# Storing a convolution's results group by group, with one transfer for both regions of an image

## The reference

```python
xn = group_norm(x)                       # 32 groups of 2 channels
pooled = xn.mean(axis=(2, 3))
a = relu(pooled @ fc1_w.T + fc1_b)
att = softmax(a @ fc2_w.T + fc2_b)       # four weights for each image
agg_w = einsum('bk,koihw->boihw', att, weight)   # an own 3x3 kernel for each image
agg_b = att @ bias
out = x + conv3x3(xn, agg_w) + agg_b     # stride 1, padding 1
```

## Time and profile before

| | |
|---|---|
| median of three runs | 313.08 us (312.87 to 314.52) |
| the profiled execution | 314.18 us |
| its span in the trace | 312.3 us |
| TensorE, products | 297.9 us busy, 95% of the span |
| TensorE, weight loads | 266.2 us, 85% |
| VectorE | 246.5 us, 79% |
| ScalarE | 189.8 us, 61% |
| GpSimd | 22.9 us, 7% |
| bytes moved by DMA | 53.62 MB, 172 GB/s over the span |

### The profile page before, as it was taken

How to read it: one execution, slowest core, us unless ns; L and a number is a source line. 1 busy time by engine, 2 the same in 40 slices (tenths; PEclk the granted TensorE clock), 3 DMA queues, 4 the chain that set the end, 5 groups by cost and what they waited for, 6 DMA issues and landing times.

```text
span 312.3 us, 15651 instructions
## 1 busy us (share of the span) xinstructions
PE 297.9 (95%) x7029; PEld 266.2 (85%) x7029; DVE 246.5 (79%) x760; ACT 189.8 (61%) x241; POOL 22.9 (7%) x32
## 2 busy tenths in 40 slices
PE   7299998999999999999999999999999999999994
PEld 5256866778787989999987998899999999999993
DVE  2988897888999998999798989889696987856000
ACT  1292937739194676738386868767684866767321
POOL 1004040040400000000000000000000000000000
PEclk9779999999999999999999999999999999999999
DMA  7893084480946658482936869495664416070564
GB/s 254 329 395 108 2 266 150 121 290 13 279 139 221 197 171 245 135 250 58 295 106 185 233 161 238 128 240 176 173 188 136 135 35 178 2 195 18 144 171 105
DMA packets 19283, 53.62 MB, mean 172 GB/s; under 512 B 7568, under 2 KB 10896, under 8 KB 19216
## 3 DMA queue, kind: packets, MB, share of 16 engines
q1 hardware_dynamic: 18912, 52.41, 56.6%
q10 hardware_dynamic: 304, 0.22, 0.3%
HBM read 26.89 MB, written 25.69 MB: 168 GB/s over the span
## 4 chain that ended last, share of the span: by engine, by line
PE 75%; DVE 10%; ACT 8%; issue 3%; DMA 2%; SPq 0%; DVEq 0%; ACTq 0%
PE acc L793 75%; DVE stats L324 2%; ACT o L675 2%; DMA x<-x 2%; DVE mix L436 2%; ACT xh L623 2%; ACT x L605 2%; ACT wh L653 1%; DVE xl L512 1%; ACT xh L631 1%; ACT wh L640 0%; DVE wparts L343 0%; DVE x L520 0%; DVE mix L434 0%; DVE mv L332 0%
## 5 line engine op out<-in xcount | busy, mean ns | idle before, releaser
L793 PE MATMUL acc<-xh,wh 64*64 64x385 f16 (+3 forms) x2304 | 112.1, 326 | 1.3 <-ACT xh L623 0.7
L793 PE MATMUL acc<-xl,wh 64*64 64x385 f16 (+3 forms) x2304 | 111.1, 325 | 0.6 <-issue 0.4
L793 PE MATMUL acc<-xh,wl 64*64 64x385 f16 (+3 forms) x2304 | 110.6, 325 | 0.6 <-issue 0.6
L675 ACT ACTIVATE o<-acc,out_par 128x392 f32<-128x392 f32 x127 | 78.2, 669 | 52.9 <-PE acc L793 52.7
L793 PEld LDWEIGHTS acc<-xh,wh 64*64 64x64 f16 x2304 | 87.8, 107 | 12.0 <-ACT wh L653 1.6
L793 PEld LDWEIGHTS acc<-xl,wh 64*64 64x64 f16 x2304 | 90.9, 107 | 7.7 <-issue 1.3
L793 PEld LDWEIGHTS acc<-xh,wl 64*64 64x64 f16 x2304 | 87.8, 107 | 10.2 <-issue 1.0
L324 DVE BATCH_NORM_STATS2 stats<-x 128x6 f32<-128x448 f32 x112 | 64.9, 615 | 5.2 <-DMA x<-x 5.2
L631 ACT ACTIVATE xh<-x,xof,xsc 128x1568 f16<-128x1568 f32 x24 | 40.5, 1690 | 32.3 <-DVE xof L398 32.3
L512 DVE TENSOR_TENSOR xl<-x,xh 128x1568 f16<-128x1568 f32 x28 | 49.9, 1785 | 8.1 <-ACT x L605 7.9
L436 DVE SCALAR_TENSOR_TENSOR mix<-w_sb,ex,mix 128x192 f32<-128x192 f32 (+1 forms) x72 | 44.2, 614 | 0.9
(11 more groups left out here) (60 smaller groups left out, 135.6 us busy)
## 6 DMA issues: line engine op xcount, KB each, us to landing
x<-x SPq DMA_DIRECT2D x30, 784.0 KB, 6.5
out<-o SPq DMA_DIRECT2D x30, 392.0 KB, 5.0
out<-o SPq DMA_DIRECT2D x30, 294.0 KB, 4.6
out<-o SPq DMA_DIRECT2D x44, 98.0 KB, 3.5
out_par<-par SPq DMA_DIRECT2D x64, 0.5 KB, 2.0
x<-x SPq DMA_DIRECT2D x2, 448.0 KB, 4.9
x<-x SPq DMA_DIRECT2D x3, 224.0 KB, 6.2
w_sb<-w_t SPq DMA_DIRECT2D x2, 288.0 KB, 4.9
```

The source lines that it names most:

```text
L675: nc.scalar.activation(o_sb[i][m][:, g * GN:(g + 1) * GN], acc[n % SLOTS][m][:, 0:GN], ACT.Identity, bias=out_par[i][m][:, 1:2], scale=out ...
L793: ins = nc.tensor.matmul(pixels[:, top:bottom, left:right], weights[i][halves[m], tap * C:(tap + 1) * C], window, start=start and step == ...
```

## The change

All pairs are now stored group by group. `group_of(p, g, m)` gives the two sides of one transfer: in DRAM a view of the image as eight bands, [band, channel, pixel], of which it takes the group's upper and lower band by a slice with a step; in SBUF all 128 rows of `o_sb` at the group's 392 columns. So a pair has eight stores of 128 rows x 392 pixels where it had six of 64 rows, and the last group is stored by one transfer for each image instead of two. The load of pair p+4 is cut into quarters of 784 pixels; quarter g is issued behind the stores of group g of pair p. The parameters of pair p+1 are issued between the stores of group 2 and the quarter behind them. The counts that the waits at L323 and L673 look for follow: 64 for a tile loaded in quarters, 64 for a pair's four stores of an image.

```diff
--- before.py
+++ after.py
@@ -194,17 +194,19 @@
             else:
                 engine.wait_ge(s_xh[half], p - EARLY + 1)
 
+        def group_of(p, g, m):
+
+            bands = out_d[2 * p + m].rearrange("c (b n) -> b c n", n=GN)
+            upper, lower = BANDS[0][g], GROUPS + BANDS[1][g]
+            return bands[upper:lower + 1:lower - upper], o_sb[p % 2][m][:, g * GN:(g + 1) * GN]
+
         block = ctx.enter_context(nc.Block())
 
         @block.sync
         def _(sp):
-            def load(p, half):
-                if p >= X_RING:
-
-                    for n in range(2):
-                        sp.wait_ge(s_xl[n], p - X_RING + 1)
+            def first_load(p, half):
                 pixels = slice(half * HALF, (half + 1) * HALF)
-                sp.dma_start(x_sb[p % X_RING][:, pixels], x_d[p, :, pixels]).then_inc(x_in[p % X_RING], 16)
+                sp.dma_start(x_sb[p][:, pixels], x_d[p, :, pixels]).then_inc(x_in[p], 16)
 
             def spread_params(p):
                 i = p % 2
@@ -213,23 +215,17 @@
                     for r in range(2):
                         sp.dma_start(out_par[i][m][halves[r], :], par[i][halves[m], :]).then_inc(s_outp[i], 16)
 
-            def store(p, m):
-                i = p % 2
-                sp.wait_ge(s_res, 2 * GROUPS * p + 2 * (GROUPS - 1) + m + 1)
-                image = out_d[2 * p + m]
-
-                sp.dma_start(image[:, 0:GN], o_sb[i][m][halves[0], HALF - GN:HALF]).then_inc(stored[i][m], 16)
-                sp.dma_start(image[:, GN:HALF], o_sb[i][m][halves[0], 0:HALF - GN]).then_inc(stored[i][m], 16)
-                sp.dma_start(image[:, HALF:PIX], o_sb[i][m][halves[1], :]).then_inc(stored[i][m], 16)
+            def load_quarter(p, n):
+
+                for half in range(2):
+                    sp.wait_ge(s_xl[half], p - X_RING + 1)
+                pixels = slice(n * HALF // 2, (n + 1) * HALF // 2)
+                sp.dma_start(x_sb[p % X_RING][:, pixels], x_d[p, :, pixels]).then_inc(x_in[p % X_RING], 16)
 
             def store_group(p, g):
-                i = p % 2
                 for m in range(2):
                     sp.wait_ge(s_res, 2 * GROUPS * p + 2 * g + m + 1)
-                    for r in range(2):
-                        first = r * HALF + BANDS[r][g] * GN
-                        sp.dma_start(out_d[2 * p + m, :, first:first + GN],
-                                     o_sb[i][m][halves[r], g * GN:(g + 1) * GN]).then_inc(stored[i][m], 16)
+                    sp.dma_start(*group_of(p, g, m)).then_inc(stored[p % 2][m], 16)
 
             for n, (first, last) in enumerate(PIECES):
                 pixels = slice(first * CHUNK, last * CHUNK)
@@ -241,30 +237,22 @@
             sp.wait_ge(s_weights[0], 16)
             for p in range(1, X_RING):
                 for half in range(2):
-                    load(p, half)
+                    first_load(p, half)
             spread_params(0)
-            for p in range(PAIRS - 1):
-
-                if p + X_RING < PAIRS:
-                    load(p + X_RING, 0)
-                spread_params(p + 1)
-                if p + X_RING < PAIRS:
-                    load(p + X_RING, 1)
-                for m in range(2):
-                    store(p, m)
-            for g in range(GROUPS - 1):
-                store_group(last_pair, g)
+            for p in range(PAIRS):
+
+                for g in range(GROUPS if p < last_pair else GROUPS - 1):
+                    store_group(p, g)
+                    if g == 2 and p < last_pair:
+                        spread_params(p + 1)
+                    if p + X_RING < PAIRS:
+                        load_quarter(p + X_RING, g)
             i, g = last_pair % 2, GROUPS - 1
             sp.wait_ge(s_res, 2 * GROUPS * PAIRS - 1)
-            for r in range(2):
-                first = r * HALF + BANDS[r][g] * GN
-                sp.dma_start(out_d[2 * last_pair, :, first:first + GN],
-                             o_sb[i][0][halves[r], g * GN:(g + 1) * GN]).then_inc(stored[i][0], 16)
+            sp.dma_start(*group_of(last_pair, g, 0)).then_inc(stored[i][0], 16)
             for i in range(2):
                 for m in range(2):
-                    pairs = PAIRS // 2
-                    total = 48 * pairs if i != last_pair % 2 else 48 * (pairs - 1) + 32 * GROUPS
-                    sp.wait_ge(stored[i][m], total)
+                    sp.wait_ge(stored[i][m], 16 * GROUPS * PAIRS // 2)
 
         @block.gpsimd
         def _(pool):
@@ -320,7 +308,7 @@
                                 dve.wait_ge(x_piece[n], 16)
                     elif t == start:
 
-                        dve.wait_ge(x_in[p % X_RING], 32 * (p // X_RING + (p % X_RING != 0)))
+                        dve.wait_ge(x_in[p % X_RING], 64 * (p // X_RING) + 32 * (p % X_RING != 0))
                     ins = nc.vector.bn_stats(stats[:, t, :], x_sb[p % X_RING][:, t * CHUNK:(t + 1) * CHUNK])
                 if end == CHUNKS:
                     ins.then_inc(s_stats, 1)
@@ -670,7 +658,7 @@
                         if m == 0:
                             act.wait_ge(s_outp[i], 64 * (p // 2 + 1))
                         if p >= 2:
-                            act.wait_ge(stored[i][m], 48 * (p // 2))
+                            act.wait_ge(stored[i][m], 16 * GROUPS * (p // 2))
                     act.wait_ge(s_conv, 2 * n + m + 1)
                     nc.scalar.activation(o_sb[i][m][:, g * GN:(g + 1) * GN], acc[n % SLOTS][m][:, 0:GN], ACT.Identity,
                                          bias=out_par[i][m][:, 1:2], scale=out_par[i][m][:, 0:1]).then_inc(s_res, 1)
@@ -748,10 +736,7 @@
                         results(p, g)
                     results(p, GROUPS - 1, (0,))
                     act.wait_ge(s_res_last, 1)
-                    for r in range(2):
-                        first = r * HALF + BANDS[r][GROUPS - 1] * GN
-                        act.dma_start(out_d[2 * p + 1, :, first:first + GN],
-                                      o_sb[p % 2][1][halves[r], HALF - GN:HALF]).then_inc(stored[p % 2][1], 16)
+                    act.dma_start(*group_of(p, GROUPS - 1, 1)).then_inc(stored[p % 2][1], 16)
 
         @block.tensor
         def _(pe):
```

## The result

| | before | after |
|---|---|---|
| median | 313.37 us (4 runs, 312.87 to 314.52) | 642.38 us (4 runs, 641.95 to 642.98) |
| ratio | | 2.050, 95% interval 2.042 to 2.058 |
| span of the profiled execution | 312.3 us | 640.7 us |
| TensorE busy | 297.9 us, 95% | 332.8 us, 52% |
| mean granted TensorE clock | 0.989 | 0.762 |

The kernel takes twice as long. The same bytes move, and TensorE has the same 7029 matrix instructions; only the stores' transfers, the cut of the loads and their order differ. The page of the changed kernel, in the parts that answer to the earlier trace rows: busy tenths in 40 slices, the chain by engine, and the DMA issues with their size and the median us to landing (the stores have none).

What follows compares the result with a forecast made beforehand. TensorE's products bound the kernel before; after, two DMA engines would. Start 29.9, fixed part 2.1, stores 641.4, loads 50.9, parameters 2.4 make 726.7 us of span, 727.5 us forecast; range 560 to 955 us.

Steps and rivals of the forecast that it cites:

- The mechanism: Merged stores: DRAM side begins with a 2, so all 128 share the same two DMA engines; chance 0.84.
- The engines stay fed: Two store engines: 44.3 us of work a pair against TensorE's 17.76, so they never run dry.
- The cover: When the next pair's parameters land, group 3's two stores and a load quarter remain queued: 11 us of work.
- The price of a packet: Merged stores: each 1568 B packet takes 78.3 ns on its engine, 641.4 us for 128 stores of 64 packets.
- both bounds of the price: Store packet at 60.2 ns gives 575 us, at 105 ns 946 us; these set the range 560 to 955.
- the line through two load rates: Packet price from two load stretches: 34.5 ns per 1000 B plus about 24 ns fixed, 78.3 ns at 1568 B.
- the 105 ns of the small stores before: High bound of a packet's price, from 64-row stores on 16 engines; put down to a queue at the SBUF ports.
- The low bound of 60.2 ns: Price of a 1568 B store packet at the loads' rate of 26.0 GB/s for each busy engine.
- The loads' term: Loads of pairs 4 to 15 on the two store engines: 4.24 us a pair, 50.9 us for twelve.
- The DMA share: Sign in the profile after: mean share near 0.15 and about 75 GB/s, flat over all slices.
- The clock: TensorE's clock may fall from 2.4 to 1.2 GHz; a pair then takes 35.5 us, below 44.3, so costs nothing.
- The rival of sixteen engines: Merged stores are spread over all sixteen engines and stay behind the products: 312.5 us, not slower; chance 0.12.

Runs made afterwards that it cites:

- e2: As e1, but the DRAM side of each 64-row store is a view [2, 32, 392], channels in another order: 643.91 us.
- e3: As e1, but the DRAM side of each 64-row store is a view [4, 16, 392], channels in another order: 370.82 us.
- e10: As e1, but the DRAM side of each 64-row store is a view [8, 8, 392], channels in another order: 313.75 us.
- e4: As e1, but the DRAM side of each 64-row store is a view [16, 4, 392], channels in another order: 320.29 us.
- e1: The changed kernel with its new order, each merged store issued as two 64-row transfers with channels outermost: 314.66 us, ratio 1.005 to the kernel before.
- e5: The kernel before, with only the last pair's 16 small stores replaced by 8 merged ones: 337.61 us against 313.85, ratio 1.077.
- e6: The changed kernel with the next pair's parameters issued ahead of a pair's stores instead of behind those of group 2: 651.69 us.
- e7: The changed kernel with groups 1 and 2 of an image stored by one transfer [2, 64, 784], 3136 B packets: 618.30 us.
- e8: The changed kernel with each quarter of a load cut into two transfers of 392 pixels, 1568 B packets: 644.12 us.
- e9: The changed kernel with all stores [2, 64, 392] issued by GpSimd, behind its step for the next pair: 423.75 us.

## Why the prediction was right, and where it missed

**The mechanism** was right: the outermost 2 sets the number of engines (e2, e3, e10, e4), the merged stores alone do it (e1, e5), and the loads and parameters queue behind them.

**The engines stay fed**, as forecast. Stretches of the changed kernel (us, busy of five engines, clock, DMA share, GB/s):

```profile
320.00:322.00 2.00, 0.00 (x0) 0.00 (x0) 0.00 (x0) 0.00 (x0) 0.00 (x0) 0.50 0.13 46
...
328.00:330.00 2.00, 0.00 (x0) 0.00 (x0) 0.00 (x0) 0.00 (x0) 0.00 (x0) 0.50 0.64 208
...
332.00:334.00 2.00, 0.00 (x0) 0.00 (x0) 0.00 (x0) 0.61 (x2) 0.00 (x0) 0.50 0.13 47
...
553.90:588.50 34.60, 20.51 (x432) 13.31 (x432) 4.40 (x3) 10.06 (x12) 0.00 (x0) 0.80 0.14 47
```

In these rows the share doesn't fall below the 0.13 of two engines, not even while all compute engines stand still at 320 us. The cover was as said: when the parameters land at 333.4 us, group 3's two stores are still under way, and SP issues the next at 334.82. e6 confirms it from the other side. SP's issues, put at 9.6 us a pair, take nearly all of the period instead (the timeline above), but that is time in which the stores ahead are moving.

**The price of a packet is the term that was mis-sized.** The chain's waits for the parameters give the period (start us, us, what):

```profile
209.43 7.40 DMA out_par<-par
...
248.27 7.41 DMA out_par<-par
...
518.47 7.95 DMA out_par<-par
...
553.89 7.54 DMA out_par<-par
588.48 7.95 DMA out_par<-par
```

With loads the landings, 216.83 and 255.68 us, are 38.85 us apart. Without loads they are 526.42, 561.43 and 596.43, twice 35.0 us. By 512 packets 35.0 us is 68.4 ns, with the parameters' small part in it, where the prediction took 78.3. The starts of the last two waits are only 34.6 us apart, which is where the 67.6 ns of the expectations came from, but those of the two before are 35.4, so this was a choice of interval and not the period.

With it the sum reads 29.9 + 2.1 for the start and one store's fixed part, 16 x 35.0 = 560.0 for the stores with their parameters and 12 x 3.85 = 46.2 for the loads: 638.2 us for a measured span of 640.7, 2.5 us short. The forecast was 85.1 us above the 642.4 measured: 83.8 us lie in the stores and parameters (641.4 + 2.4 against 560.0) and 4.7 us in the loads, less 3.4 us that the other terms were short. The time is inside the range because the range went by both bounds of the price.

The step that failed is the line through two load rates. Its fixed part of 24 ns came from the stretch 3 to 7 us, near the start of the traffic, and e7 gives 12 ns for stores, e8 some 5 ns for loads. That stretch isn't the five pieces of x alone either: SP issues the weights at 4.9 us, so the mean packet of 2509 B was itself a guess. Why the stretch is slower wasn't tried.

At the other end, the 105 ns of the small stores before isn't the cost of one packet on its engine: e2 reads 64-row tiles at the low price. The prediction put it down to all 16 engines reading the same 64 rows, with the Trainium skill's eight ports ("SBUF — State Buffer", "Door 1: The DMA port swizzle (why `[64,N]` ≈ `[32,N]`)"). e4 speaks against that as the whole cause. Its stores read the same 64 rows by the same 16 engines as e1's, and only the order on the DRAM side differs. The stretch from 296 to 306 us, stores and parameters alone, in e1 and then in e4:

```profile
296.00:306.00 10.00, 10.00 (x252) 10.00 (x248) 0.00 (x0) 3.75 (x6) 0.00 (x0) 1.00 0.52 123
```

```profile
296.00:306.00 10.00, 10.00 (x248) 8.30 (x244) 0.00 (x0) 3.17 (x6) 0.00 (x0) 1.00 0.29 92
```

That is 123 / (0.52 x 16) = 14.8 GB/s for each busy engine in e1, as before the change, and 92 / (0.29 x 16) = 19.8 GB/s in e4, some 106 and 79 ns a packet. To the full share e4's rate would be 92 / 0.29 = 317 GB/s, well over the page's 218, so the side in DRAM has a part in the price. Which part wasn't tried. The low bound of 60.2 ns, for which that page spoke, is 8.2 ns from the measured 68.4, the value taken 9.9.

**The loads' term** was 4.24 us a pair; measured 38.85 - 35.0 = 3.85 us, or 120 ns for a packet of 3136 B where the line gave 132.4. The low rate, 26.0 GB/s for each engine, would have given just that.

**The DMA share** was put near 0.15 and 75 GB/s over the whole span. It is that only where no loads are left (0.14, 47 GB/s); from 209.4 to 248.2 us, with them, it is 0.27, and 84 GB/s are the mean. The sum had the loads, the sign to look for left them out.

**The clock.** It fell to 0.5 in the idle stretches (row 320.00), and the products took 332.8 us of busy time for 297.9. As forecast it costs nothing: they took 20.51 of 34.60 us in the last row shown. The reason given for it is thinner than it looked, since the 35.5 us of a pair at half the clock is no longer below a period of 35.0. What helps is that much of the low clock falls into idle time: over that row the clock is 0.80.

**The rival of sixteen engines** is what e1 and e10 show when its condition is met by other means: 314.66 and 313.75 us, no gain over before. So by the prediction's own estimate even a merged store on all engines would have had nothing to win here but the last half microsecond; no run has one. The rival's count of issues, 16 a pair, was for merged stores; e1 has 24, 14.4 us of SP in 17.76.

## What to carry to other kernels

Before two transfers are merged into one, look at the outermost dimension of both sides: here a 2 there meant two engines and a 4 four, and the one issue saved by merging cost most of the bandwidth. In these profiles it shows as a flat DMA share near k/16 with few GB/s, while every engine waits for small transfers that stand behind the large ones; don't follow the name in the wait, count the share. A row of equal landings is a better clock than the starts of waits: one interval of these, picked from several, gave a price and a term for the loads that seemed exact and weren't. And where stores are off the path, as here, their form is a risk without a gain.

## What the runs showed of the hardware that was not expected

- SP is held at the issue while stores are ahead: in e5 a store's issue takes 3.8 us on average (22.77 / 6) and the last 4.32 us, about the 64 x 68.4 ns = 4.38 us that one store needs on its engine, where an issue is some 0.60 us with room. I read it as a queue that is full and takes a store when one leaves; its length isn't shown. The long issues are a symptom.
- What stores cost when all 16 engines read the same 64 rows depends on the order in DRAM: 14.8 GB/s for each busy engine with channels in order (e1), 19.8 with every sixteenth channel together (e4).
- Two engines reading from the same 64 rows are as fast as two that read from one half each (e2, 643.91 us against 642.38).
- The same transfer from GpSimd's queue isn't bound to one pair of engines (e9), but has 368 packets for 128 rows (47104 / 128).
